# One product for queries and keys per pair of images in a windowed-attention block: 64 rows by 128 columns, and a new order within the quarters

## What is computed

```python
xn = layernorm(x.transpose(0, 2, 3, 1), norm1_g, norm1_b)
xw = window_partition(roll(xn, (-SHIFT, -SHIFT)), WS)
q, k, v = split(xw @ qkv_w.T + qkv_b)
attn = softmax(q * hd ** -0.5 @ k.T + bias + mask)     # mask: -100 between regions of a shifted window
x = x + window_reverse((attn @ v) @ proj_w.T + proj_b)
y = layernorm(x, norm2_g, norm2_b)
y = dwconv3x3(pin_w @ y); x = x + pout_w @ (gelu(y[:h]) * y[h:])
# then the graph block: 1x1 convolutions, a maximum over shifted rows and columns, gelu, an MLP
```

## Time and profile before

| | us |
|---|---|
| median of the runs | 267.8 |
| the profiled execution | 267.85 |
| its span, first to last instruction | 265.9 |
| TensorE busy (share of the span) | 252.4 (95%) |
| weight loads busy (beside the products) | 158.1 (59%) |
| VectorE busy | 176.6 (66%) |
| ScalarE busy | 165.1 (62%) |
| POOL busy | 131.1 (49%) |
| mean DMA rate | 93 GB/s |

### The profile page before, as it was taken

One profiled execution on the slowest core, in us unless ns is written; L12 is line 12 of the kernel. 1 busy time (PEld: TensorE's weight loads), 2 busy tenths in 40 slices (PEclk: granted clock), 3 DMA queues, 4 the chain that ended last, 5 costly groups with the idle time before them and its releaser, 6 DMA issues.

```text
span 265.9 us, 5129 instructions
## 1 busy us (share of the span) xinstructions
PE 252.4 (95%) x1894; PEld 158.1 (59%) x1894; DVE 176.6 (66%) x371; ACT 165.1 (62%) x244; POOL 131.1 (49%) x149
## 2 busy tenths in 40 slices
PE   8888999999999999999998999999999999999981
PEld 8777878789697896978887544333442233222210
DVE  3884787768688686785878573465794245788322
ACT  4899779587786877858624533255343535596771
POOL 8984816116767477642187999402141000208732
PEclk9999999999999999999999999999999999999997
DMA  6901000020020167402573177457312000104312
GB/s 209 247 10 30 2 2 2 0 71 21 21 71 4 48 222 306 141 2 54 210 294 99 33 274 256 121 192 234 108 30 59 1 0 4 30 0 104 91 44 59
DMA packets 11470, 24.64 MB, mean 93 GB/s; under 512 B 6473, under 2 KB 8337, under 8 KB 10582
## 3 DMA queue, kind: packets, MB, share of 16 engines
q1 hardware_dynamic: 9006, 21.91, 25.3%
q0 software_dynamic: 1280, 1.97, 3.2%
q10 hardware_dynamic: 1160, 0.44, 0.7%
HBM read 18.41 MB, written 3.15 MB: 81 GB/s over the span
## 4 chain that ended last, share of the span: by engine, by line
PE 76%; DVE 13%; ACT 5%; issue 2%; DMA 1%; POOL 1%; POOLq 0%; DVEq 0%; ACTq 0%
PE psum L771 11%; PE psum L647 11%; PE psum L772 10%; PE psum L656 9%; PE psum L676 5%; DVE diff L1174 5%; DVE mx L1172 5%; PE psum L851 3%; PE psum L821 3%; PE psum L780 3%; PE psum L837 3%; PE psum L788 3%; PE psum L811 2%; PE psum L608 2%; PE psum L693 2%
## 5 line engine op out<-in xcount | busy, mean ns | idle before, releaser
L1172 DVE TENSOR_REDUCE mx<-psum 128x6 f32<-128x384 f32 x64 | 35.3, 552 | 26.3 <-PE psum L647 26.3
L647 PE MATMUL psum<-kmv,stq 128*128 128x192 f32 x256 | 47.0, 327 | 0.4 <-ACT stq L954 0.4
L1292 DVE TENSOR_TENSOR gated<-psum,gel 64x512 f32<-64x512 f32 x32 | 22.1, 693 | 33.6 <-ACT gel L1052 33.3
L647 PEld LDWEIGHTS psum<-kmv,stq 128*128 128x128 f32 x256 | 40.8, 190 | 0.5 <-ACT stq L954 0.5
L1052 ACT ACTIVATE gel<-psum 64x512 f32<-64x512 f32 x32 | 18.9, 591 | 35.3 <-PE psum L772 33.0
L496 POOL TENSOR_TENSOR rstd<-var,power 128x16 f32<-128x16 f32 x7 | 20.5, 2924 | 34.5 <-DVE var L1154 34.0
L988 ACT ACTIVATE pt<-psum 128x768 f32<-128x768 f32 x32 | 26.0, 811 | 18.6 <-PE psum L656 18.3
L1174 DVE TENSOR_TENSOR diff<-psum,mx 128x384 f32<-128x384 f32 x64 | 35.7, 557 | 2.2
L771 PE MATMUL psum<-sta,pk 108*128 108x512 f32 x64 | 34.0, 612 | 0.0
L676 PEld LDWEIGHTS psum<-val,pt 128*64 128x64 f32 x768 | 25.0, 137 | 13.9 <-issue 12.2
L772 PE MATMUL psum<-stb,pk 108*128 108x512 f32 x64 | 32.7, 592 | 0.0
(11 more groups left out here) (126 smaller groups left out, 395.8 us busy)
## 6 DMA issues: line engine op xcount, KB each, us to landing
sta<-scratch SPq DMA_DIRECT2D x12, 576.0 KB
stb<-scratch SPq DMA_DIRECT2D x12, 576.0 KB
xtok<-xt SPq DMA_DIRECT2D x8, 192.0 KB, 3.4
xin<-xw SPq DMA_DIRECT2D x8, 192.0 KB, 5.3
out<-yo POOLq DMA_DIRECT2D x28, 48.0 KB, 1.9
x<-x1s SPq DMA_DIRECT2D x24, 48.0 KB
pk<-pack SPq DMA_DIRECT2D x1, 714.5 KB, 7.3
scratch<-ytok SPq DMA_DIRECT2D x3, 192.0 KB, 2.2
```

What stands on the lines that cost most here:

```text
L647: l = mm(s[:, NH * WT * p:NH * WT * (p + 1)], stq[:, m % 2, p, 2 * pair + w, :], kmv[:, m % 2, p, 2 * pair + w].rearrange("k h n -> k (h n ...
L1172: v.tensor_reduce(mx[:, slot, w, :], groups, AX.X, ALU.max).then_inc(max_ready, 1)
L1292: v.tensor_tensor(gated[64 * (b % 2):64 * (b % 2) + 64, c * CH:(c + 1) * CH], bank(conv_bank(u))[64:128], gel[:, u % 4, :], ALU.mult).then ...
```

## The change

Each pair of images has its own 64 rows of `xhat` and `xs`: 48 rows of two images, then 16 rows (`MARK` to `PR`) with the one for the bias, the four region marks and zeros. The marks are part of `xhat` now: they come with the weights, are copied once into each of two `xhat` buffers (VectorE for the first, POOL for the second), and are turned with the rest, so `turn_xhat` has weights of 128 columns, not 96, and the DMA of `feat` into `xs` falls away. Queries and keys of a chunk are made by one function, `make_qk`: for each pair of images one product with 64 rows and 128 columns (64 columns of queries, 64 of keys) into a bank of its own, 6 or 7. It stands where `make_q` stood, in quarter 3, and takes over the wait of `make_k`. The first chunk is made as before. The out turn moves from quarter 2 to the end of quarter 1, behind `mix`, and waits for the keys to be taken; the projection moves from quarter 3 to quarter 2. On ScalarE the four query and six key activations stay, in another order; on VectorE `residual` moves ahead of `divide`, and the second norm's variance behind the subtraction of quarter 3.

```diff
 PACK = {
-    "eye": (128, 128), "wq": (KX, 128), "wk": (KX, 128), "wv": (KX, BC), "scales": (128, 4),
-    "vecs": (BC, 2), "vecs_g": (128, 5), "vecs_x": (128, 12),
-    "rpb": (128, NH * WT),
+    "eye": (128, 128), "wq": (128, 128), "wk": (128, 128), "wv": (128, BC), "scales": (128, 4),
+    "vecs": (128, 2), "marks": (128, 2 * TOK * (PR - MARK)), "vecs_g": (128, 5), "vecs_x": (128, 12),
+    "rpb": (128, NH * WT), "wqk": (128, 128),
...
-        xhat = sb(att, "xhat", [128, TOK, BC])
-        xs = sb(att, "xs", [KX, 2, CH])
+        xhat = sb(att, "xhat", [128, 2, TOK, 2 * PR])
+        xs = sb(att, "xs", [128, 2, CH])
...
+        QK = (6, 7)
+
+        def keys_of(p, h, par):
+            src = own_rows(1)
+            return (kmv[own_rows(p), par, p, :, h, :], bank(QK[p])[src].rearrange("k (w n) -> k w n", n=WT),
+                    wt("scales", h, h + 1)[src])
+
+        def queries_of(p, j, par):
+            src = slice(32 * j, 32 * j + 32)
+            return (stq[64 * p + 32 * j:64 * p + 32 * j + 32, par, p, :, WT * j:WT * j + WT],
+                    bank(QK[p])[src].rearrange("k (w n) -> k w n", n=WT), wt("scales", 3, 4)[src])
...
-            sp.dma_start(xs[BC:KX, :, :], feat.rearrange("k (i n) -> k i n", i=2)).then_inc(rows_in, 16)
...
             pool.wait_ge(filled, 1)
+            g.tensor_copy(*marks_of(1)).then_inc(marks_ready, 1)
             first_norm(1)
...
-            def make_q(m):
+            def make_qk(m):
+
                 pe.wait_ge(xs_ready, m + 1)
-                mm(bank(6), wt("wq"), xs[:, m % 2, :], start=True, stop=True).then_inc(q_made, 1)
-
-            def make_k(m):
                 wait(pe, x1s_ready, m - 2)
-                mm(bank(7), wt("wk"), xs[:, m % 2, :], start=True, stop=True).then_inc(k_made, 1)
+                for p in range(2):
+                    rows = own_rows(p)
+                    l = mm(bank(QK[p]), wt("wqk")[rows], xs[rows, m % 2, :], start=True, stop=True)
+                l.then_inc(qk_made, 1)
 
             def make_v(m, at=6):
-                wait(pe, stq_ready, m)
+                wait(pe, bank_taken, m)
...
             def turn_out(m):
 
                 pe.wait_ge(ot_ready, 2 * m + 2)
+                if m + 2 < NCH:
+                    pe.wait_ge(kmv_ready, m + 2)
...
                         scores(m + 1, l - 2)
-                    if l == 0 and not last:
-                        make_k(m + 1)
...
-                        if l == 2 and m >= 1:
-                            turn_out(m - 1)
-                        if l == 2 and m + 2 < NCH:
-                            pe.wait_ge(val_ready, m + 2)
-                            turn_xhat(m + 2)
-                        if l == 3:
-                            if m + 2 < NCH:
-                                make_q(m + 2)
-                            if m >= 1:
-                                project(m - 1)
+                    if l == 1 and last:
+                        turn_out(m - 1)
+                    if l == 2 and m >= 1:
+                        project(m - 1)
+                    if l == 2 and m + 2 < NCH:
+                        pe.wait_ge(val_ready, m + 2)
+                        turn_xhat(m + 2)
+                    if l == 3 and m + 2 < NCH:
+                        make_qk(m + 2)
...
                     mix(m, l)
+                    if l == 1 and m >= 1 and not last:
+
+                        turn_out(m - 1)
...
                 for l in range(4):
+                    if l == 0 and not last and m:
+                        take_k(m + 1, 0, 1)
+                    if l == 2 and m >= 1 and not last:
+                        take_out(m - 1)
                     if not last or l < 3:
                         exps(4 * m + l + 1)
                     if l == 0 and not last:
-                        take_k(m + 1, 0)
+                        if not m:
+                            take_k(m + 1, 0)
+                        take_q(m + 1, 1)
...
                     if l == 3 and m + 2 < NCH:
-                        take_q(m + 2)
+                        take_q(m + 2, 0)
+                        take_k(m + 2, 0, 0, 1)
...
             a(*positions_of(1, 1), ACT.Copy).then_inc(positions_ready, 1)
-            take_q(1)
+            take_q(1, 0)
             square(0, 2)
...
                 ahead(2)
+                if m >= 1:
+                    residual(m - 1)
                 divide(m, 0)
-                if last:
-                    residual(m - 1)
-                elif m >= 2:
+                ahead(3)
+                if m >= 2 and not last:
                     variance(1, m - 2)
-                ahead(3)
-                if not last and m >= 1:
-                    residual(m - 1)
...
+            dve.wait_ge(first_in, 16)
+            v.tensor_copy(*marks_of(0)).then_inc(marks_ready, 1)
             first_normalise()
```

More of the change, by code:

```diff
@@ L24 @@
 NREG = 4
-KX = BC + 1 + NREG
+PR = 64
+MARK = G2
 TOK = CH // 128
@@ L58, with build @@
 RING = 4
-def build(nc, xw, xt, feat, pack, out):
+def build(nc, xw, xt, pads, pack, out):
     scratch = nc.dram_tensor("scratch", [B, PAD + C * NT + PAD], F32, kind="Internal").ap()
@@ L180, in build @@
         x1_stored = [sem(f"x1_stored{par}") for par in range(2)]
-        q_made, k_made, stq_ready, kmv_ready = (sem(n) for n in ("q_made", "k_made", "stq_ready", "kmv_ready"))
+        qk_made, bank_taken, stq_ready, kmv_ready = (sem(n) for n in ("qk_made", "bank_taken", "stq_ready", "kmv_ready"))
         v_made, val_ready = sem("v_made"), sem("val_ready")
@@ L238, in keys_of, with first_keys_of @@
+        FIRST_K, FIRST_Q = (7, 4), (6, 3)
+        def first_keys_of(p, h, half):
             rows = own_rows(p)
-            return (kmv[rows, par, p, w0:w1, h, :],
-                    bank(at, WT * (w1 - w0))[rows].rearrange("k (w n) -> k w n", n=WT), wt("scales", h, h + 1)[rows])
-        def queries_of(r, par, at=6, w0=0, w1=WS):
+            return (kmv[rows, 0, p, 4 * half:4 * half + 4, h, :],
+                    bank(FIRST_K[half], 4 * WT)[rows].rearrange("k (w n) -> k w n", n=WT), wt("scales", h, h + 1)[rows])
@@ L243, in queries_of, with first_queries_of @@
+        def first_queries_of(r, half):
             p, j = divmod(r, 2)
             rows = slice(32 * r, 32 * r + 32)
-            return (stq[rows, par, p, w0:w1, WT * j:WT * j + WT],
-                    bank(at, WT * (w1 - w0))[rows].rearrange("k (w n) -> k w n", n=WT), wt("scales", 3, 4)[rows])
-        FIRST_K, FIRST_Q = (7, 4), (6, 3)
+            return (stq[rows, 0, p, 4 * half:4 * half + 4, WT * j:WT * j + WT],
+                    bank(FIRST_Q[half], 4 * WT)[rows].rearrange("k (w n) -> k w n", n=WT), wt("scales", 3, 4)[rows])
@@ L615, in turn_xhat @@
                 for k in range(TOK):
-                    l = nc.tensor.transpose(bank(at)[0:BC, 128 * k:128 * k + 128], xhat[:, k, :], wt("eye"))
+                    l = nc.tensor.transpose(bank(at)[:, 128 * k:128 * k + 128], xhat[:, m % 2, k, :], wt("eye"))
                 l.then_inc(xs_turned, 1)
@@ L705, in attend @@
                         scores(m + 1, l - 2)
-                    if l == 0 and not last:
-                        make_k(m + 1)
+                    if l == 0 and last:
+                        pe.wait_ge(cen2_ready, m - 2)
+                        turn_x1(m - 2)
                     if l == 1 and not last:
@@ L942, in take_q @@
                     act.wait_ge(queries_zeroed, m + 1)
-                for r in range(4):
-                    dst, src, own = queries_of(r, m % 2)
+                for j in range(2):
+                    dst, src, own = queries_of(p, j, m % 2)
                     l = a(dst, src, ACT.Copy, scale=own)
-                l.then_inc(stq_ready, 1)
+                if p:
+                    l.then_inc(stq_ready, 1)
             def take_first_q():
@@ L952, in take_first_q, with take_k @@
                     for r in range(4):
-                        dst, src, own = queries_of(r, 0, FIRST_Q[half], 4 * half, 4 * half + 4)
+                        dst, src, own = first_queries_of(r, half)
                         l = a(dst, src, ACT.Copy, scale=own)
                     l.then_inc(first_queries, 1)
-            def take_k(m, p):
-                act.wait_ge(k_made, m)
+            def take_k(m, p, h0=0, h1=NH):
+                act.wait_ge(qk_made, m)
                 wait(act, scores_made, WS * (m - 1))
-                for h in range(NH):
+                for h in range(h0, h1):
                     dst, src, own = keys_of(p, h, m % 2)
                     l = a(dst, src, ACT.Copy, scale=own)
-                if p:
-                    l.then_inc(kmv_ready, 1)
+                if h1 == NH:
+                    l.then_inc((bank_taken, kmv_ready)[p], 1)
             def take_v(m, at=6):
@@ L1001, in attend @@
                         square(1, m - 2)
-                    if l == (1 if last else 2) and m >= 1:
+                    if l == 1 and last:
                         take_out(m - 1)
```

(25 more changed lines are left out.)

60 lines of the change are left out of this document (29 added, 31 removed).

## The result

The changed kernel takes 269.0 us (median of six runs, 268.93 to 269.21), the kernel before 267.8 in the same comparison: a ratio of 1.0046, with a 95% interval of 1.0035 to 1.0057. It is 1.2 us slower, for a forecast of 1.6 and a range of 267.4 to 271.3. The profiled execution took 269.21 us with a span of 267.2, 1.3 above that of before.

A forecast was written before the change was run, and what follows sets the result against it. The prediction took TensorE's queue to bound the attention part, with a VectorE floor per quarter. Terms -0.1 + 0.1 + 0.7 + 0.4 + 0.5 = +1.6 gave 269.4 us, range 267.4 to 271.3.

The forecast's parts named there:

- likeliest case: Whole kernel: the main forecast, +1.6 us to 269.4 us, own range 268.3 to 270.5; chance 0.62.
- step 3: Order of work in chunks 2 to 5: quarter 0 loses the keys but stays at 3.82 us; +0.17 us a chunk.
- step 1: Quarter 3: two 0.86 us products become one pair on two array halves, taking 1.06 us; bounds 0.86 and 1.92.
- the pair does not overlap: Rival for the query and key products: 1.92 us in place of 1.06, +0.86 in seven places, about 275; chance 0.05.
- step 2: Turn of xhat with 128 weight columns in place of 96: 0.54 us, +0.10 a chunk; bounds 0.44 and 0.58.
- Quarters 1 and 2: Chunks 2 to 5: out turn adds 0.43 us to quarter 1; projection replacing out turn adds 0.48 to quarter 2.
- Chunk 6: No xhat turn and no pair there, so it only pays the out turn in quarter 1: +0.4 us.
- The start: Chunk 0: an earlier second exponential gains 0.5 us, mostly given back later; net -0.1, bounds -0.5 and +0.3.
- The second norm: Later variance delays POOL's power, the last y and ScalarE's gelus, so the output product: +0.5 us, bounds 0 and +0.8.
- ScalarE in quarter 0: ScalarE's evacuations and exponential end at 16.41 us, before the next turn may start at 16.81: hidden by 0.4.
- weight loads are covered: Rival: loads hide under scores; pair under 0.91 us, xhat turn 0.44, total 267.4 to 267.9, not slower; chance 0.25.

The follow-up runs named there:

- the spare product: Changed kernel with one more 128-row, 128-column product in quarter 0 of chunks 0 to 6, into an unread bank: 269.07 us.
- Both edits that take the wait away: Changed kernel with the last y stored by SP instead of ScalarE, or with VectorE's old order in chunk 6 alone: 268.66 us each.
- the one without the wait: Changed kernel with VectorE's old order in chunk 6 and the values product moved to quarter 0, except in chunk 0: 265.86 us.

## Why the prediction was right, and where it was off

Its likeliest case happened, by its own steps; the size was over by 0.4 of 1.6 us, and the term that was mis-sized is the wider turn, 0.10 us in each of five chunks.

- *The floor and quarter 0* (step 3, "no gain"): right. Quarter 0 took 3.89 us in place of 3.90, the idle time is the 0.91 us that VectorE's chain leaves, and the spare product shows that it is free.
- *The pair* (step 1, 1.06): right. 1.06 with both halves, 1.06 with one, 1.82 for two full products. The step from `scores` to `mix` is 0.21 above that of a plain product, so the late stage's 0.20 for a change of shape held here too. The Trainium skill, page TensorEngine Tiling (Array Packing), section Key Properties, says that changing the tiling mode drains TensorE. The 0.21 us agree with that, though no run shows what TensorE does in them. The rival "the pair does not overlap" is out.
- *The wider turn* (step 2, +0.10): wrong. The xhat turn takes 0.53 us to `mix` with weights of 96 columns (97.39 to 97.92) and 0.53 with 128 (98.31 to 98.84). I had divided the chain's 0.80 for a `turn` of six behind `mix` by six, 0.134. But part of that 0.80 belongs to the end of `mix`: behind the out turn the same six take 0.66 from start to start (95.49 to 96.15), 0.11 each, which is also the step of the 96-wide ones, 0.44 for the four of the out turn in the kernel before (96.95 to 97.39):

```profile
96.95 0.60 PE L684 MATMUL psum<-pk,ot 128*96 128x128 f32 x4
```

The chain gives a piece the time from the end of the one before, not from start to start as was said ahead of the prediction, and that is not its cost where shapes change.
- *Quarters 1 and 2* (+0.43 and +0.48): counted by the ends, as in the forecast, they came out at +0.56 and +0.23. The out turn behind `mix` took 0.58 for 0.44 (95.08 to 95.66) and the `turn` behind it 0.65 for 0.80. These two errors cancel, as both come from the same 0.14 us at the end of `mix`, which the chain gives to whatever piece stands behind it. The sum was right there without the forecast having seen this. What is left is the 0.10 of the wider turn, and this is the difference of the settled chunk, +0.06 for +0.17. Over four chunks +0.30 us came of the 0.7 forecast. In chunk 1, from 40.98 to 57.27, it is the same 0.10 again: 0.03 shorter than before, where I had +0.1.
- *Chunk 6* (+0.4): right, 0.64 less 0.22.
- *The start* (-0.1): right in sum, -0.05, but not in every part. The second exponential came early enough for `turn` at 24.44 (forecast 24.5, before 25.03). Quarters 1 and 2 of chunk 0 gave back 0.5 us and not 0.2 to 0.3, as `scores`, due at 29.05, waited for the keys till 29.48. The pair in quarter 3 cost 0.09 for 0.15.
- *The second norm* (+0.5): right in mechanism, and nearly in size. POOL's power started at 137.42 (137.9 forecast), the last `y` came at 167.52 (168.1), the output product waited about 0.4 us. Both edits that take the wait away gain 0.34.
- *ScalarE in quarter 0* ("hidden by 0.4"): right. Order of time, ScalarE, changed kernel:

```profile
104.32 1.83 ACT L989 ACTIVATE kmv<-psum,pk 64x512 f32<-64x512 f32 x3
106.18 0.81 ACT L1015 ACTIVATE pt<-psum 128x768 f32<-128x768 f32 x1
```

The exponential ends at 106.99, 0.5 before the `turn` of 107.52, and reading the upper half of a bank into either half of `kmv` costs no more than the 1.83 us for three of the earlier trace rows.

One sentence of the prediction stands on a row that its group lacks, that the thin first chunk keeps the clock at 1.00 with a microsecond of idle in it. It is this one, busy time by stretch, kernel before:

```profile
25.00:41.00 16.00, 14.94 (x168) 12.75 (x168) 11.64 (x35) 12.69 (x21) 8.32 (x5) 1.00 0.01 2
```

Its idle time comes in pieces of at most half a microsecond. In the changed kernel the longest piece of that stretch is 1.28 us, and the clock stayed at 1.00 there too:

```profile
40.98 0.87 PE L684 MATMUL psum<-pk,diff 128*128 128x128 f32 x6 [1.28 <-DVE diff L1206]
```

The general form that I gave it, that an idle quarter does not slow the clock, is too wide: in the run that moved the values in chunk 0, the traced execution has 1.81 us of idle time in one piece and then a granted clock of 0.50.

The rival "weight loads are covered" was half right for a different reason. Its xhat turn at 0.44 did happen (by the ends; 0.53 from start to `mix` in both kernels), but its other half, a pair under 0.91, did not, and by its own condition it falls.

## What to carry to other kernels

Where a loop's stages each have a floor set by another engine, the busy share of the bound engine over the whole loop says nothing about what a saving is worth: ask in which stage the work goes away, and whether that stage was already at its floor. Here TensorE lost 5.4 us of busy time and the kernel was 1.2 us slower: what left quarter 0 became idle time, while the out turn and the projection went to quarters above the floor, and the last `y` came late, with ScalarE's gelus behind its store. Moving other work into quarter 0, from chunk 1 on, gained 2.8 us. A cheap test of a floor is a spare instruction in that stage: if it is free, removing as much gains nothing.

## What the runs showed that I had not expected

Transposes of fp32 take 0.11 us each whether their weights have 96 or 128 columns. Between products of 128 rows, one product of 64 rows costs as much as two side by side (1.16 us from the end of `scores` to `mix`), 0.21 more than one of 128 rows, so half the array alone is dearer than all of it. And after 1.81 us of idle time in one piece the clock was at 1.2 GHz for some 3 us (from between 26 and 28 us to 30 us) in the execution that was profiled, while by their mean clocks seven of the ten executions of that kernel kept it up. Median against median, that run is 1.4 us behind the one without the wait (267.22 against 265.86).
